# Dots and oz matmuls interleaved in a causal attention loop, with four accumulators open at once

## The reference

```python
xn = layernorm(x)
q, k, v = xn @ Wq.T, xn @ Wk.T, xn @ Wv.T          # per head [T, 128]
q = feature_map(q) * 128 ** -0.5                    # layernorm(q * gamma + beta)
k = feature_map(k)
attn = tril((q @ k.T) ** 2)
o = (attn @ v) / (attn.sum(-1) + EPS)
x + o @ Wo.T + FFN(xn)      # FFN: fwht(silu(xn@W1.T) * (xn@W3.T)) @ W2.T
```

## Time and profile before

| what | us |
|---|---|
| time, median of 2 runs (6200.1 and 6581.27) | 6390.69 |
| time of the profiled execution | 6200.1 |
| its span (core 7, the slowest) | 6198.5 |
| PE matmul busy | 4755.1 (77%) |
| DVE busy | 1179.7 (19%) |
| ACT busy | 1070.7 (17%) |

### The profile page before, as it was taken

The page is one execution under the profiler, slowest core; times in us unless marked ns, Lnnn a source line. Parts: engine busy times, 40 slices in busy tenths (PEclk is TensorE's granted clock), DMA queues, the critical chain, the costliest instruction groups (busy, mean ns, idle before and its releaser), DMA issues.

```text
span 6198.5 us, 68932 instructions; the slowest of 8 cores (6169.0 to 6198.5 us)
## 1 busy us (share of the span) xinstructions
PE 4755.1 (77%) x23090; PEld 2241.4 (36%) x23090; DVE 1179.7 (19%) x2744; ACT 1070.7 (17%) x1939; POOL 119.5 (2%) x220
## 2 busy tenths in 40 slices
PE   2334667667766775675789999999999989787877
PEld 0001243324332532342334444444444434333333
DVE  5664123213211321132110000000000000000000
ACT  0001215321522252234001111111111110000000
POOL 0000000000000000000000000000000000000000
PEclk9999886778677767876889999999999999898988
DMA  7674110121012001102542222222222236656654
GB/s 188 191 196 105 41 28 15 35 51 18 11 41 45 15 15 45 38 11 63 144 143 52 54 59 52 60 53 60 52 58 55 53 107 181 196 170 183 182 174 146
DMA packets 238169, 524.74 MB, mean 85 GB/s; under 512 B 18694, under 2 KB 108806, under 8 KB 227590
## 3 DMA queue, kind: packets, MB, share of 16 engines
q10 hardware_dynamic: 91392, 218.13, 11.7%
q0 software_dynamic: 46464, 117.45, 11.6%
q1 hardware_dynamic: 99974, 184.74, 9.1%
HBM read 528.65 MB, written 109.05 MB: 103 GB/s over the span
## 4 chain that ended last, share of the span: by engine, by line
PE 67%; DMA 11%; DVE 9%; ACT 5%; issue 4%; another core or an unknown queue 1%; SPq 1%; ACTq 1%; DVEq 1%; POOL 0%; POOLq 0%
PE ps_g L910 14%; PE ps_u L918 14%; PE ps_o L1042 14%; PE ps_y L477 7%; PE ps_y L599 4%; PE ps_rb L647 4%; PE ps_ao L851 3%; PE ps_oz L718 2%; DMA w2pp_scr<-foldst 2%; DVE foldst L265 2%; DMA wslab<-wq 2%; DMA wslab<-wk 2%; DMA out<-outst 2%; ACT attnS L653 1%; ACT ych L512 1%
## 5 line engine op out<-in xcount | busy, mean ns | idle before, releaser
L1042 PE MATMUL ps_o<-w2sl,u_sl 128*128 128x512 bf16 x4096 | 904.5, 384 | 202.3 <-DVE outst L1066 164.6
L910 PE MATMUL ps_g<-xnT,w1sl 128*128 128x512 bf16 x4096 | 928.5, 380 | 13.4 <-DMA w3sl<-w 13.4
L918 PE MATMUL ps_u<-xnT,w3sl 128*128 128x512 bf16 x4096 | 925.8, 379 | 0.0
L1042 PEld LDWEIGHTS ps_o<-w2sl,u_sl 128*128 128x128 bf16 x4096 | 403.0, 99 | 703.8 <-issue 236.6
L910 PEld LDWEIGHTS ps_g<-xnT,w1sl 128*128 128x128 bf16 x4096 | 401.3, 98 | 499.0 <-issue 17.5
L918 PEld LDWEIGHTS ps_u<-xnT,w3sl 128*128 128x128 bf16 x4096 | 400.8, 98 | 483.3
L477 PE MATMUL ps_y<-xnT,wslab 128*128 128x512 bf16 x2048 | 543.1, 429 | 2.7 <-issue 2.3
L938 DVE TENSOR_TENSOR hidst<-silust,ps_u 128x512 bf16<-128x512 f32 x256 | 175.9, 687 | 1665.0 <-ACT silust L933 1665.0
L949 ACT ACTIVATE ust<-ps_uh 128x512 bf16<-128x512 f32 x256 | 152.9, 597 | 1489.6 <-PE ps_uh L944 1489.6
L647 PE MATMUL ps_rb<-ybq,ybk 128*128 128x512 bf16 x640 | 314.2, 541 | 73.1 <-ACT attnS L653 31.8
L517 PE MATMUL ps_rb<-ych,onedm_s 128*128 128x512 bf16 x128 | 59.0, 461 | 405.7 <-ACT ych L512 405.7
(11 more groups left out here) (92 smaller groups left out, 2398.9 us busy)
## 6 DMA issues: line engine op xcount, KB each, us to landing
w2sl<-w2pp_scr ACTq DMA_DIRECT2D x256, 512.0 KB, 4.2
w2pb<-w2p SPq DMA_DIRECT2D x32, 1024.0 KB, 7.6
w2pp_scr<-foldst ACTq DMA_DIRECT2D x128, 256.0 KB, 6.6
w1sl<-w POOLq DMA_DIRECT2D x64, 512.0 KB, 5.5
w3sl<-w POOLq DMA_DIRECT2D x64, 512.0 KB, 7.7
u_scr<-ust SPq DMA_DIRECT2D x256, 128.0 KB, 1.7
u_sl<-u_scr SPq DMA_DIRECT2D x32, 1024.0 KB, 14.7
w2pb<-w2p POOLq DMA_DIRECT2D x32, 512.0 KB, 8.1
```

The lines of the kernel that those rows point to most:

```text
L910: em.op("tensor", lambda e, cb=cb, bb=bb, dc=dc, tc=tc: e.matmul(ps_g[cb][:], w1sl[bb][:, dc * 128:(dc + 1) * 128], xnT[:, dc * T + tc * 5 ...
L918: pv3 = em.op("tensor", lambda e, cb=cb, bb=bb, dc=dc, tc=tc: e.matmul(ps_u3[cb][:], w3sl[bb][:, dc * 128:(dc + 1) * 128], xnT[:, dc * T + ...
L1042: pv = em.op("tensor", lambda e, ttl=ttl, dd5=dd5, wb=wb, hb=hb, hq=hq: e.matmul(ps_o[ttl * 2 + dd5][:], u_sl[:, hb * 512 + ttl * 128: hb ...
```

## The change

Within a group PE no longer does all dots first. After dots(j) it does oz(j − 1): the up to four matmuls that use the square of key block j − 1, one for each query tile il ≥ j − 4c. So the four accumulators of a group are all open from its first to its last key block. For that:

- attnS becomes three buffers of 512 columns, taken in turn (r = j % 3), where it was one of 16 x 512; a square waits until oz(j − 3) has used its buffer.
- The eight PSUM banks are named pb 0 to 7. ps_y is pb 0 and 1, ps_rb pb 2 to 4, and the accumulators of tiles 0 to 3 are pb 5, 6, 7 and 0.
- The first oz of a group waits until all four accumulators have been read out by the onat of the group before.
- Every oz matmul raises the PE semaphore; before, only the stops did.
- The four stops stand together at the group's end, then the four sets of zt, rec and onat (four onat buffers, before two), and all four transposes come between dots 1 and 2 of the next group. They use the ps_rb banks in turn with the dots (rbc counts both), where they used ps_y.
- attn0b is squared and masked directly in bfloat16; the float32 attn0f and its cast are gone.

The core of it:

```diff
-    attnS = gsb("attnS", [128, NTT * 512], BF16)
+    attnS = [gsb(f"attnS_{i}", [128, 512], BF16) for i in range(3)]
-    onat = [gsb(f"onat_{i}", [128, 128], BF16) for i in range(2)]
+    onat = [gsb(f"onat_{i}", [128, 128], BF16) for i in range(4)]
-    ps_y = [gps(f"ps_y_{i}", [128, 512]) for i in range(2)]
-    ps_rb = [gps(f"ps_rb_{i}", [128, 512]) for i in range(3)]
-    ps_oz = [gps(f"ps_oz_{i}", [128, 129]) for i in range(3)]
+    pb = [gps(f"pb_{i}", [128, 512]) for i in range(8)]
+    ps_y = [pb[0], pb[1]]
+    ps_rb = [pb[2], pb[3], pb[4]]
+    ps_oz = {0: pb[5], 1: pb[6], 2: pb[7], 3: pb[0]}
...
+                def emit_ozb(j, hl=hl, c=c):
+                    r = j % 3
+                    lo = max(0, j - 4 * c)
+                    em.wait("tensor", *gtok(f"aS{j % 3}" if not (c == 0 and j == 0)
+                                            else "attn0f_rdy"))
...
+                    if j == 0:
+                        for il in range(4):
+                            em.wait("tensor", *gtok(f"pb{ozbank[il]}"))
...
+                        pv = em.op("tensor", lambda e, il=il, r=r, j=j, hl=hl: e.matmul(
+                            ps_oz[il][:, 0:129],
+                            attnS[r][:, il * 128: il * 128 + 128],
+                            vaug[:, j * (GH * 129) + hl * 129:
+                                 j * (GH * 129) + hl * 129 + 129],
+                            start=(j == 0), stop=False, skip_group_check=True),
+                            s_pe)
...
+                for j in range(nj):
+                    if j == 2 and pending_post:
+                        for fn in pending_post:
+                            fn()
+                        pending_post[:] = []
+                    emit_dots(j)
+                    if j >= 1:
+                        emit_ozb(j - 1)
+                emit_ozb(nj - 1)
                 for il in range(4):
-                    pv_oz_last = emit_oz(il)
-                    if il >= 1:
-                        emit_post_dve(il - 1)
-                    if il >= 2:
-                        emit_post_tr(il - 2)
-                emit_post_dve(3)
+                    pv_grp = emit_stop(il)
+                for il in range(4):
+                    emit_post_dve(il)
```

More of the change, by code:

```diff
@@ L540, in build_program @@
                 em.wait("tensor", *gtok(f"wlo_rdy{wb}"))
[L541 removed]
+                em.wait("tensor", *gtok("pb6"))
                 pv = None
@@ L571, in build_program @@
             em.wait("tensor", s_act, vark_done)
-            em.wait("tensor", *gtok("ps_oz0"))
+            em.wait("tensor", *gtok("pb5"))
             pv = None
@@ L637, in build_program, with emit_dots @@
                 nj = 4 * c + 4
[L638 to L646, removed]
+                def emit_dots(j, hl=hl, c=c):
+                    db = rbc[0] % 3
+                    rbc[0] += 1
+                    r = j % 3
+                    em.wait("tensor", *gtok(f"pb{2 + db}"))
                     pv = em.op("tensor", lambda e, db=db, hl=hl, j=j, c=c: e.matmul(
@@ L731, in build_program @@
-                post_dv = {}
-                def emit_post_dve(il, c=c, hl=hl, g=g):
-                    ob = il % 3
-                    pv = oz_pv[il]
+                        em.wait("scalar", *gtok("aSfree0"))
+                        av = em.op("scalar", lambda e, db=db: e.activation(
+                            attnS[0][:, 128:512], ps_rb[db][:, 128:512],
+                            AF.Square), s_act)
+                        tok[f"pb{2 + db}"] = (s_act, av)
+                        tok["aS0"] = (s_act, av)
@@ new lines, in emit_dots @@
+                        em.wait("tensor", *gtok(f"pb{2 + db}"))
+                        pv = em.op("tensor", lambda e, db=db, hl=hl: e.matmul(
+                            ps_rb[db][:, 0:128], yk0f[:, hl * 128:(hl + 1) * 128],
+                            yq0f[:, hl * 128:(hl + 1) * 128],
+                            start=True, stop=True), s_pe)
+                        em.wait("scalar", s_pe, pv)
+                        em.wait("scalar", *gtok("attn0b"))
+                        av = em.op("scalar", lambda e, db=db: e.activation(
+                            attn0b[:], ps_rb[db][:, 0:128], AF.Square), s_act)
@@ new lines, in emit_stop, with emit_post_dve @@
+                def emit_stop(il, hl=hl, c=c):
+                    i = 4 * c + il
+                    pv = em.op("tensor", lambda e, il=il, hl=hl, i=i: e.matmul(
+                        ps_oz[il][:, 0:129],
+                        varq_row[0:1, hl * T + i * 128: hl * T + i * 128 + 128],
+                        ecol[:], start=False, stop=True, skip_group_check=True),
+                        s_pe)
+                    oz_stop_pv[il] = pv
+                    return pv
+                def emit_post_dve(il, hl=hl, c=c):
+                    pv = oz_stop_pv[il]
+                    pr = il
@@ L787, in build_program @@
                 em.op("sync", lambda e: e.dma_start(
-                    out=dbg_d["oTg"], in_=oTg[0][:]), s_dbg2, 16)
+                    out=dbg_d["oTg"], in_=oTg[:]), s_dbg2, 16)
                 tok["oTgS2"] = (s_dbg2, 0)
```

197 lines of the change are left out of this document (85 added, 112 removed).

## The result

The changed kernel is slower: 1.0316 times the time of the kernel before, 95% interval 1.0288 to 1.0343, from runs of 6393 to 6426 us against 6197 to 6230. The forecast was 1.030 (6387 against 6200.1). In 8 of the 14 runs of the changed kernel (6523 to 6979 us) and in 6 of the 12 of the kernel before (6454 to 6829) one or both dies ran at a lower clock, and the ratio leaves these out; with those runs in, the medians are 6666.69 us and, before, 6342.35 us, and the first of them lies above the range that was given, 6305 to 6465.

The account below looks back on a forecast made before the run. Before, ACT bounds the dots part and PE the oz part. Interleaved, 16 heads at 61 us make 976 against 789.1 us, +187 on 6200: 6387 us, 3.0% slower, range 6305 to 6465.

Parts of the forecast that it names:

- The inner loop: Mid-group round of square, oz and dots: 1.93 or 1.52 us per two steps at 1.2 or 2.4 GHz.
- The group boundary: From a group's last square to the next group's square(2), across four read-outs: 8.8 or 8.2 us, three times per head.
- The head: Inner loop, three boundaries and head's change together: 65.0 us at 1.2 GHz, 56.7 at 2.4, middle 61 taken.
- The head's change: Boundary between two heads, transposes drained before the first dots: 10.7 us at 1.2 GHz, 9.9 at 2.4.
- The clock: PE in attention, between 1.2 and 2.4 GHz: the middle taken, 61 us per head, both ends kept.
- The all-1.2 rival: PE stays at 1.2 GHz in attention: 65.0 us per head, +251, 6451 us; chance 20%.
- The overlap: Rival at the oz(0) wait: hidden oz wins, not slower, 6121 us or 6075 with the loop at ACT's 0.69; 8%.
- No measurable change: Rival: attention at 2.4 GHz nearly throughout with shorter edges, +118 us or less, about 6315; chance 9%.
- Increments: Rival: semaphore increments or extra waits on PE cost half to all of 64 us more, 6419 to 6451; 8%.
- the base: Starting time of the whole kernel: the profiled execution's own 6200.1 us, to which attention's +187 us was added.

Follow-up runs that it names:

- x2_short_chain: Changed kernel with zt left out, the reciprocal taken straight from the accumulator's sum column (EPS*EPS*HD not added): 6332 to 6337 us, mean window 230.5 us.
- x7_tr_first: Changed kernel with the four transposes of the group before put ahead of the first oz, after dots(1): 6366 to 6439 us, mean window 236.7 us.
- x8_dbuf: Changed kernel with two accumulator sets in turn, the four read-outs waiting for the group's last stop: 6361 to 6380 us, ratio 1.0260 to the kernel before.
- x4_one_inc: Changed kernel with the PE semaphore raised only by the last oz matmul of each step: 6414 to 6463 us, mean window 247.6 us.
- x3_look2: Changed kernel with PE one dots matmul further ahead, dots(j) then oz(j-2): 6287 to 6306 us, mean window 214.8 us.
- x5_all: Changed kernel, one accumulator set, dots two ahead, stop and read-out after each tile's last oz, one transpose per step: 6193 to 6280 us.
- x9_dbuf_look2: Changed kernel with two accumulator sets, dots two ahead, transposes one per step from step 3 of the next group: 6142 to 6185 us.
- x10_carry: Two accumulator sets, dots two ahead, spread transposes, plus two oTg buffers and read-outs and transposes carried over a head's change, against changed kernel: 6127 to 6186 us.

## Why the prediction was right, and where it was wrong

*Direction and size.* +3.16% measured, +3.0% forecast. Attention grew by 201 us on core 7 against 187.

*The inner loop.* Right: 1.91 and 1.50 us for two steps against 1.93 and 1.52, and 24.4 us per head against 25.1, the middle of 27.9 and 22.2.

*The group boundary.* Right, and shown to be the cause. From the last square to the end of the fourth onat it is 6.20 us; the sum had 6.36 and 6.21 with 0.11 to PE in them, so 6.25 and 6.10. From there to square(2) it is 2.53; the sum had 0.11 + 0.43 + 1.13 + 0.90 = 2.57 and 0.11 + 0.23 + 1.06 + 0.69 = 2.09. Three of them make 26.3 us per head against 25.5. x2_short_chain moved the first part alone and got back what it shortened; x7_tr_first and x8_dbuf worked on the second.

*The head.* Medians from head to head are 61.9 us against 61 forecast and 49.5 before. The head's change, from the last square to the third of the next head, takes 11.0 us where the sum had 10.7 at 1.2 GHz and 9.9 at 2.4, so it was the one part priced too low at either clock, by little. That 61 came so near is in part luck: by the middle of the two clocks the inner loop was 0.7 us too dear, and the three boundaries 0.8 and the head's change 0.7 too cheap. The PE's idle ahead of oz for onat was put at near 170 us and is 182.7.

*The clock.* The middle of the two levels was a choice. The granted clock in the windows is 0.65 to 0.68, where it was 0.63 to 0.66, so about a third of the time is at 2.4 GHz, and not the half that the middle stands for. The sum's own ends weighted so give (2 × 65.0 + 56.7)/3 = 62.2 us per head, nearer to the measured 61.9 than the middle was. The all-1.2 rival (65.0 us per head) is excluded.

*The rivals.* The overlap did not win: it needed the chain to be over in 1.3 us, and it takes 4.39. "No measurable change" is excluded by the interval. Increments cost nothing that shows (x4_one_inc).

*What was wrong: the base.* The failing step is this one: "it is one of two runs whose median is 6390.69, so I work from its own time". The two runs shown, 6200.1 and 6581.27, already said that a median of all runs can lie anywhere between the two. The range of 6305 to 6465 was built from attention's costs alone, and took in nothing for that. What was measured in its place: more than half of the changed kernel's runs took 6523 us or more, so the median of all 14, 6666.69, lies outside the range and 280 us above the forecast, while the runs that the ratio uses, 6393 to 6426, lie within it and 6 to 39 us above the forecast. The forecast of the difference held; that of the median of all runs had no ground.

*Smaller misses, all in the experiments.* For x3_look2 I took ACT's 0.69 us as the pace once three squares are in flight and overlooked PE's own 0.86 at 1.2 GHz; it gained more than expected only by what it did to the transposes and at the start of a head. For x5_all I let the gains add and left out that the single set of accumulators still holds the first oz, 87.4 us in all, wherever square(2) stands.

## What to carry to other kernels

Before interleaving two phases, follow the buffers that the merged phase keeps open: if they are the same from group to group, whatever empties them stands between the groups. Here that is 4.4 us of small DVE work four times per head, more than the 8 to 15 us of matmuls per head that were hidden. A wait taken away in an ordered list can be found again at the next instruction that needs the same result (with a second set the 182.7 us at oz fell to 15.0, and the 63.6 at the transposes rose to 156.1), so second buffers paid little, 52 us, until what stood behind the wait had a new place too. And with more blocks in flight the round of square, oz and dots is divided by their number (1.93 or 1.52 us by two), but not below the busiest engine's own work at the clock that it gets: with three it was 0.86 us by PE at 1.2 GHz and 0.69 by ACT at 2.4.

## What the runs showed of the hardware that was not expected

Raising a semaphore with each of 2176 matmuls or with 640 of them made no difference (windows of 247.5 and 247.6 us). Four one-row stops in a row are cheap: from the first of them to the dots behind the fourth it is 0.32 us (the rows at 1718.30 and 1718.62), where in the kernel before the next matmul started 0.21 or 0.15 us after each single one. The granted clock in the attention windows does not simply follow how much PE stands still: in the kernel before PE was idle for 40 to 43 us of a window, at 0.63 to 0.66; in the changed kernel for over 100, at 0.65 to 0.68; in x9_dbuf_look2 for 51 to 52, at 0.73 to 0.74; in x10_carry for 46 to 49, at 0.76 to 0.80. What sets it wasn't tried, nor how much of the gain of the last two is due to it.
